# A gated norm and column-scan kernel: the first states, the copies for the median, and the sums at both ends

## What is computed

```
x = x + gate0(gn(x)); x = x + gate1(gn(x)); x = x + gate2(gn(x))   # gn: 32 groups of channels
# gate: mean, max, std of each (image, channel) plane; med = the median of these 3072 values of an image
#   z = sum_k((u - med)**3 * cfc_w) / sqrt(1 + eps) * bn_w + bn_b;  return x * sigmoid(z)
x = x + scan(gn(x))
# scan, step: y = Wc @ prev + conv_b;  y = where(y >= 0, y, prelu_a * y);  cur = y + x_i
#   over the columns forwards (31 steps), then backwards over the result (31 steps)
```

## Time and profile before

| what | us |
|---|---|
| median of three runs | 862.54 (862.22 to 862.80) |
| the profiled execution, its own time | 862.8 |
| its span | 861.1 |
| TensorE busy | 837.6 (97%) |
| VectorE busy | 660.2 (77%) |
| ScalarE busy | 413.6 (48%) |
| GpSimd busy | 67.7 (8%) |

### The profile page before, as it was taken

How to read it: one execution, slowest core, us unless ns; L and a number is a source line. 1 busy time by engine, 2 the same in 40 slices (tenths; PEclk the granted TensorE clock), 3 DMA queues, 4 the chain that set the end, 5 groups by cost and what they waited for, 6 DMA issues and landing times.

```text
span 861.1 us, 13814 instructions
## 1 busy us (share of the span) xinstructions
PE 837.6 (97%) x4062; PEld 662.6 (77%) x4062; DVE 660.2 (77%) x1461; ACT 413.6 (48%) x1375; POOL 67.7 (8%) x106
## 2 busy tenths in 40 slices
PE   7888899999999999999999999999999999999998
PEld 6743478888888888888888888888888888888886
DVE  6977887776766767677776778778787888778887
ACT  6964324544454444544445444544445444454444
POOL 8963300000000000000000000000000000000000
PEclk9999999999999999999999999999999999999999
DMA  9940200000000000000000023332233313332233
GB/s 375 418 188 0 98 26 1 0 0 0 0 0 0 0 0 0 0 0 0 0 0 0 30 68 97 97 97 65 81 97 97 94 58 92 97 97 81 66 97 98
DMA packets 70654, 56.34 MB, mean 65 GB/s; under 512 B 1904, under 2 KB 66416, under 8 KB 68720
## 3 DMA queue, kind: packets, MB, share of 16 engines
q1 hardware_dynamic: 70640, 56.17, 19.6%
HBM read 39.39 MB, written 16.78 MB: 65 GB/s over the span
## 4 chain that ended last, share of the span: by engine, by line
PE 88%; POOL 5%; DVE 4%; ACT 1%; issue 1%; POOLq 0%; DVEq 0%
PE ps_prods L677 27%; PE ps_prods L683 27%; PE ps_prods L680 27%; PE ps_turns L699 6%; POOL pairs L401 3%; ACT stage L500 1%; DVE below_flags L1027 1%; DVE cells L1040 0%; PE ps_below L598 0%; PE ps_values L629 0%; PE ps_group L640 0%; POOL stage L394 0%; POOL stage L397 0%; PE ps_second L662 0%; DVE gate L1082 0%
## 5 line engine op out<-in xcount | busy, mean ns | idle before, releaser
L677 PE MATMUL ps_prods<-w_hi,s_hi 128*128 128x512 f32 (+1 forms) x1000 | 404.6, 405 | 0.2 <-DVE s_hi L1178 0.2
L680 PE MATMUL ps_prods<-w_lo,s_hi 128*128 128x512 f32 (+1 forms) x1000 | 402.7, 403 | 0.0
L683 PE MATMUL ps_prods<-w_hi,s_lo 128*128 128x512 f32 (+1 forms) x1000 | 392.7, 393 | 0.0
L527 ACT ACTIVATE act_buf<-ps_prods 128x256 f32<-128x256 f32 x247 | 81.6, 383 | 352.8 <-PE ps_prods L683 352.8
L1129 DVE SCALAR_TENSOR_TENSOR x_sb<-act_buf,x_sb 128x256 f32 (+1 forms) x247 | 105.2, 426 | 153.6 <-ACT act_buf L534 143.5
L677 PEld LDWEIGHTS ps_prods<-w_hi,s_hi 128*128 128x128 f32 x1000 | 188.4, 188 | 39.5 <-DVE s_lo L1184 1.4
L683 PEld LDWEIGHTS ps_prods<-w_hi,s_lo 128*128 128x128 f32 x1000 | 188.8, 189 | 38.5 <-DVE s_lo L1184 0.2
L680 PEld LDWEIGHTS ps_prods<-w_lo,s_hi 128*128 128x128 f32 x1000 | 189.1, 189 | 32.3
L534 ACT ACTIVATE act_buf<-ps_turns,bias 128x128 f32<-128x128 f32 x494 | 157.0, 377 | 51.6 <-PE ps_turns L699 51.6
L540 ACT ACTIVATE ps_below<-ps_turns,neg_bias 128x128 f32<-128x128 f32 x494 | 152.4, 362 | 0.0
L1136 DVE SCALAR_TENSOR_TENSOR x_sb<-ps_below,neg_slope,x_sb 128x256 f32 (+1 forms) x247 | 118.8, 481 | 5.4
(11 more groups left out here) (198 smaller groups left out, 346.0 us busy)
## 6 DMA issues: line engine op xcount, KB each, us to landing
stage<-x_cols SPq DMA_DIRECT2D x31, 512.0 KB, 4.0
out_cols<-x_sb SPq DMA_DIRECT2D x31, 512.0 KB, 4.8
x_sb<-x_cols SPq DMA_DIRECT2D x15, 1024.0 KB, 19.8
w_raw<-w_t SPq DMA_DIRECT2D x8, 512.0 KB, 19.2
x_sb<-x_cols SPq DMA_DIRECT2D x1, 2048.0 KB, 8.1
x_sb<-x_cols SPq DMA_DIRECT2D x2, 512.0 KB, 27.1
out_cols<-x_sb SPq DMA_DIRECT2D x4, 128.0 KB, 2.1
params<-gates SPq DMA_DIRECT2D x1, 60.0 KB, 14.4
```

The lines of the kernel that those rows point to most:

```text
L527: act.activation(act_buf[:, half], ps_prod[c if bank is None else bank][:, half], ACT.Copy) .then_inc(raw_copied, 1)
L677: pe.matmul(out, s_hi[:, k, :], w_hi[:, k, w_cols], start=(k == 0), stop=False)
L680: pe.matmul(out, s_hi[:, k, :], w_lo[:, k, w_cols], start=False, stop=False)
L683: return pe.matmul(out, s_lo[:, k, :], w_hi[:, k, w_cols], start=False, stop=(k == CT - 1))
```

## The change

The new kernel does these things:

- **Sums of the last tile in parts.** GpSimd adds the first half of the last tile in two pieces too, and TensorE takes each as it comes. ScalarE squares image 0 of the last tile over the columns that landed first, then its last quarter, so there are 33 square passes; VectorE adds the two sums.
- **Copies.** ScalarE makes copies(0) once unit 0 is there, VectorE copies(1) and copies(2); GpSimd none. Two small VectorE instructions of each later layer move into rounds 4 and 5 of the median, and two more of the last norm go.
- **First states.** Before the root is known, ScalarE writes x * a_scale + g_shift for tiles 0 to 5 into stage, 24 instructions of 32 numbers a partition (L541 of the new kernel; g_shift holds pull less the mean until then). VectorE does this for tiles 6 and 7 (L1236, L1238) and multiplies by the root (g_scale until then) into s_hi and stage. TensorE does the s_hi products of a pair ahead of its s_lo products. WARM_UPS is 8.
- **Last two tiles.** Their columns get slope * bias added early (L1181 new), then slope * y (L1151), then (1 - slope) * max(y + bias, 0) (L1157), where max(...) comes from ScalarE.

The diff, cut to its core:

```diff
@@
-    WARM_UPS = 10
+    WARM_UPS = 8
+    RAW_TILES = CT - 2
...
-        act_passes = 1 + N * CT
+        act_passes = 2 + N * CT
@@ block.gpsimd
-                    if ct == CT - 1 and b == 1:
+                    if ct == CT - 1 and b == 0:
+                        pair_add(ct, b, 0, 0, COLS // 4, COLS // 8)
+                        pair_add(ct, b, COLS // 8, COLS // 8, 3 * COLS // 8, COLS // 8)
+                    elif ct == CT - 1:
                         pair_add(ct, b, 0, COLS // 2, 5 * COLS // 8, COLS // 8)
...
+                pool.tensor_scalar(rest_slope[:, :], slope[:, :], -1.0, 1.0, ALU.mult, ALU.add).then_inc(signs_ready, 1)
+                pool.tensor_tensor(sloped_bias[:, :], bias[:, CT - 2:CT], slope[:, 0:1].broadcast_to([P, 2]), ALU.mult)\
+                    .then_inc(signs_ready, 1)
...
-                pool.wait_ge(unit_ready, 2 * layer + 2)
-                pool.tensor_copy(*copies(2)).then_inc(pool_copied, 1)
@@ block.scalar
+                landed = slice(0, LAST_COL if ct == CT - 1 else COLS)
+                plane_square(0, landed, squares_mean[:, 0, ct:ct + 1])
                 if ct == CT - 1:
                     act.wait_ge(x_last_loaded, 16)
-                for n in range(N):
-                    plane_sum(plane_of(n, ct), ACT.Square, squares_mean[:, n, ct:ct + 1], scale=PIX ** -0.5,
-                              bias=mean_div[:, n, ct:ct + 1])
+                    plane_square(0, slice(LAST_COL, COLS), squares_rest[:, 0:1])
+                for n in range(1, N):
+                    plane_square(n, slice(0, COLS), squares_mean[:, n, ct:ct + 1])
...
-                act.wait_ge(unit_ready, 2 * layer + 1)
-                act.activation(*copies(1), ACT.Copy).then_inc(act_copied, 1)
+                act.wait_ge(unit_ready, layer + 1)
+                act.activation(*copies(0), ACT.Copy).then_inc(act_copied, 1)
...
+            act.wait_ge(raw_ready, 1)
+            for ct in range(RAW_TILES):
+                for n in range(N):
+                    rows = slice(n * H, (n + 1) * H)
+                    last = act.activation(stage_col[:, ct, rows], x_sb[:, ct, 0, rows], ACT.Identity,
+                                          bias=g_shift[:, n, ct:ct + 1], scale=a_scale[:, n, ct:ct + 1])
+                last.then_inc(raw_normed, 1)
...
-                act.wait_ge(transposed, final * 4 + 4 + j)
-                act.activation(ps_below[:, 512 + j * P:512 + (j + 1) * P], ps_last_below[j], ACT.Relu,
-                               bias=neg_bias[:, CT - 2 + j:CT - 1 + j], scale=-1.0).then_inc(negated, 1)
+                act.wait_ge(last_turned, j + 1)
+                act.wait_ge(column_added, final * 4 + 7)
+                act.activation(ps_below[:, 512 * j:512 * j + P], ps_last_raised[j], ACT.Relu,
+                               bias=bias[:, CT - 2 + j:CT - 1 + j]).then_inc(negated, 1)
@@ block.tensor
-                    parts = 2 if ct == CT - 1 and b == 1 else 1
+                    parts = 2 if ct == CT - 1 else 1
...
-                        pe.wait_ge(dve_copied, layer + 1)
-                    elif t == 2:
                         pe.wait_ge(act_copied, layer + 1)
-                    elif t == 4:
-                        pe.wait_ge(pool_copied, layer + 1)
+                    elif t % 2 == 0:
+                        pe.wait_ge(dve_copied, 2 * layer + t // 2)
...
-                    pe.transpose(ps_last_below[j], part, ident[:, :])
-                    pe.transpose(ps_last_above[j], part, ident[:, :]).then_inc(transposed, 1)
+                    pe.transpose(ps_last_whole[j], part, ident[:, :]).then_inc(transposed, 1)
+                    pe.transpose(ps_last_raised[j], part, ident[:, :]).then_inc(last_turned, 1)
...
+            def high_products(c, k):
+                w_cols = slice(c * HALF, (c + 1) * HALF)
+                pe.matmul(ps_prod[c], s_hi[:, k, :], w_hi[:, k, w_cols], start=(k == 0), stop=False)
+                pe.matmul(ps_prod[c], s_hi[:, k, :], w_lo[:, k, w_cols], start=False, stop=False)
+
+            def low_product(c, k):
+                return pe.matmul(ps_prod[c], s_lo[:, k, :], w_hi[:, k, c * HALF:(c + 1) * HALF],
+                                 start=False, stop=(k == CT - 1))
...
+                for q in range(1, 4):
+                    pe.wait_ge(first_high, q + 2)
+                    for k in (2 * q, 2 * q + 1):
+                        high_products(0, k)
+                    pe.wait_ge(state_ready, q + 1)
+                    for k in (2 * q, 2 * q + 1):
+                        last = low_product(0, k)
@@ block.vector
+            dve.wait_ge(act_summed, act_passes - (N - 1))
+            whole = mark(dve.tensor_tensor(squares_mean[:, 0, CT - 1:CT], squares_mean[:, 0, CT - 1:CT],
+                                           squares_rest[:, 0:1], ALU.add))
             plane_means(CT - 1).then_inc(means_asked, 1)
...
+                dve.tensor_copy(*copies(1)).then_inc(dve_copied, 1)
+                after(third_unit)
+                dve.tensor_copy(*copies(2)).then_inc(dve_copied, 1)
...
-                dve.tensor_tensor(pull[:, :, :], pull[:, :, :], means, ALU.subtract)
+                dve.tensor_tensor((pull if more else g_shift)[:, :, :], pull[:, :, :], means, ALU.subtract)
...
-                    dve.tensor_tensor(a_scale[:, :, :], a_scale[:, :, :], scaled[:, :, :], ALU.add)
+                    dve.tensor_tensor(a_scale[:, :, :], a_scale[:, :, :], scaled[:, :, :], ALU.add).then_inc(raw_ready, 1)
...
+                        if layer > 0 and k == 4:
+                            dve.tensor_tensor(scaled[:, :, :], a_scale[:, :, :], grow[:, :, :], ALU.mult)
+                        if layer > 0 and k == 5:
+                            dve.tensor_tensor(a_scale[:, :, :], a_scale[:, :, :], scaled[:, :, :], ALU.add)
...
-            def first_state(ct0, cts, shifted, nth, high=None):
+            def first_state(ct0, cts, shifted, nth):
                 part = slice(ct0, ct0 + cts)
+                root = by_row(g_scale, ct0, cts)
+                if ct0 < RAW_TILES:
+                    dve.wait_ge(raw_normed, ct0 + cts)
+                dve.tensor_tensor(by_image(s_hi[:, part, :]), by_image(stage_col[:, part, :]), root, ALU.mult)\
+                    .then_inc(first_high, 1)
+                dve.tensor_tensor(by_image(stage_col[:, part, :]), by_image(stage_col[:, part, :]), root, ALU.mult)\
                     .then_inc(shifted, 1)
...
+            dve.tensor_tensor(g_shift[:, :, :], g_shift[:, :, :], g_scale[:, :, :], ALU.mult)
+            link(dve.tensor_tensor(g_scale[:, :, :], g_scale[:, :, :], a_scale[:, :, :], ALU.mult))
             dve.wait_ge(x_back, 16)
```

More of the change, by code:

```diff
@@ L808, in link @@
                 after(mark(ins))
-            unit_marks = [0]
             def root_seed(out, a):
@@ L880, in first_norm @@
                 means = ps_means.rearrange("p (n c) -> p n c", n=N)
-                after(topped)
+                after(max(topped, whole))
                 dve.wait_ge(off_ready, 2)
@@ L1139, in scan_step @@
                     nth = i * 4 + (2 * c + 5)
+                    if last and c == 1:
+                        dve.wait_ge(signs_ready, 4)
+                        col = column(w, CT - 2, 2)
+                        dve.tensor_tensor(col, col, sloped_bias[:, :].unsqueeze(2).broadcast_to([P, 2, NH]), ALU.add)\
+                            .then_inc(last_sloped, 1)
                     add_above(0)
```

128 lines of the change are left out of this document (63 added, 65 removed).

## The result

The changed kernel takes 853.95 us (853.88 to 854.02), the kernel before on the same chip 862.54 (862.22 to 863.24): a ratio of 0.9897 [0.9886, 0.9907], with the 95% interval in brackets. The prediction was 861.9 with a range of 860.2 to 862.8, so 8 us are missing in it, and the time fell outside the range.

What follows compares the result with a forecast made beforehand. From 116 us on, TensorE's back-to-back products were taken to bound the kernel. Terms 0.0 + 0.61 - 0.49 + 0.50 = 0.62 us gave 862.2 from the profiled execution, 861.9 from the median; range 860.2 to 862.8.

Steps and rivals of the forecast that it cites:

- the interval of ScalarE's instructions: First scan step: start-to-start time of ScalarE's 24 new instructions, taken as 0.29 us, bounds 0.17 and 0.43.
- the covers of the copies: Median copies: whether ScalarE's copy starts sooner than today's; 0.61 us gained if so, range 0.2 to 0.7.
- sums of the last tile: End of the statistics: earlier first piece offset by an added instruction, 0.0 us, bounds -0.1 and +0.15.
- copies: Three layers of the median: six transposes run unbroken without GpSimd's copy, gaining 0.35, 0.18 and 0.08 us.
- first step: First scan step: TensorE starts 0.5 us earlier but then waits for ScalarE, a net loss of 0.49 us.
- last step: Last scan step: last two tiles finish earlier after TensorE's last transposes, gaining 0.50 us.
- both waits: First scan step: TensorE stands about 0.8 us before tiles 2-3 and 0.8 before tiles 4-5.
- 6.18 - 23p: First step's gain in us, p being the interval of ScalarE's 24 instructions; at 0.29 it is -0.49.
- the row-based overlap: First step: profile rows gave each memory operand 0.08 us of interval, so 0.29, against the skill page's 0.306.
- The rival of a free second operand: First step: interval at or below 0.24, gaining 0.6 to 1.36 us; kernel 860.0 to 860.8; chance 0.19.
- that of no overlap: First step: ScalarE's instructions don't overlap, interval towards 0.43, where the kernel takes 865.1 us; chance 0.06.
- none of the three: Besides free operand and no overlap: ScalarE's copy no sooner, VectorE's last four instructions one by one; 862.6 us, chance 0.07.

Runs made afterwards that it cites:

- The run of the change in the old places: Changed kernel with rest_slope and sloped_bias declared behind both_shift, so s_hi, s_lo and act_buf lie as in the kernel before: 862.33 us, ratio 1.0001.
- both runs with TensorE alone: Kernel before plus four steps' products after the last addition, other engines still; old places, then states 128 bytes further: 906.3 and 894.1 us.

## Why the prediction was wrong

**The step that failed** is in its first paragraph: the scan "is TensorE's products back to back, and the change touches none of them but the last few". It holds for their waits and their number, not for their duration: the pitch fell from 232.4 to 228.9 ns, and that is the 8.7 us. No term of the sum had the pitch of the products in it, though the scan is 740 us of the 861: 1% of it is 7 us, more than the four terms together. The chances inherit it. They were spread over the interval of ScalarE's instructions and the covers of the copies, so the range was 2.6 us wide and could not hold the time, and no rival spoke of where the operands lie. The trace of before could not have given the size, since nothing in it has another place for the states. But the change declares two tensors ahead of three that TensorE reads, s_hi, s_lo and act_buf, and that they move could have been seen.

**The sum itself.** In the traces of before and after:

| term | predicted | measured |
|---|---|---|
| sums of the last tile | 0.0 | +0.13 |
| copies | +0.61 (0.35 + 0.18 + 0.08) | +0.60 (0.31 + 0.20 + 0.09) |
| stall in the second layer | none | -0.36 |
| first step | -0.49 | -0.81 |
| last step | +0.50 | +0.49 |
| sum | +0.62 | +0.05 |
| the scan between | 0 | +8.71 |

+0.05 and +8.71 make 8.76, the difference of the spans (861.05 and 852.28). The run of the change in the old places agrees, at 1.0001 [0.9992, 1.0011], though by that interval it could not tell +0.05 from +0.62. Its trace tells more: a_scale is there 0.17 earlier than before (0.37 in the changed kernel), the first step loses 0.84 and the last gives 0.50, so the last two don't come from the places.

*Copies:* right, part by part (the 0.09 of the third layer is what is left of 0.37 - 0.64 when the stall's 0.36 is taken out). *Statistics:* the first piece began at 44.01, 0.34 earlier where I had 0.27; from there to the end of the last read (48.93) lie 4.92 us in place of 4.64, so the further piece cost 0.28, where I had 0.29. VectorE then followed 0.03 behind the read in place of 0.10.

*First step:* the sign, both waits and the mechanism were right; the term mis-sized is the interval, 0.305 in place of 0.29. By the prediction's own formula 6.18 - 23p that is -0.84, measured -0.81. The trace agrees with the Trainium skill here (ScalarE: Activation LUTs, section "What ACT_TABLE_LOAD costs"), which had given 0.306 and, by the prediction, -0.88 (its own formula makes 0.306 come to -0.86); the row-based overlap that I preferred was too generous. The rival of a free second operand is refuted by the same row, and so is that of no overlap. *Last step:* right.

*Rivals:* none of the three came. The faster outcome came by a way that I had no case for.

## What to carry to other kernels

Where one engine is busy 97% of the span with thousands of like instructions, look at their pitch, not only at the waits between them: compare their count in a fixed stretch before and after. A small tensor declared ahead of the operands of a matmul shifts them, and here 64 bytes were worth 1% and 128 bytes 1.4%, more than every edit of the change together. So fix the places of loaded and streamed operands before judging any edit, try one or two placements (here the best was all four at the same place within 256 bytes), and when a diff adds or removes a tensor, undo the shift in a run of its own before crediting the edit.

## What the runs showed of the hardware

- Products of 512 columns with an fp32 128x128 load beside each follow each other every 226.8 ns or every 232.4, by the places of the operands alone, with no other engine at work. In the scan the mean pitch ran from 227.2 ns (the weights by 128 bytes) to 233.5 (s_lo and act_buf by 128).
- The old time came back when the states moved by 256 bytes. The effect is not gradual: 32 bytes beside a good place it is gone.
- The intervals repeat in short turns that run across all kinds of products: seven with the old places, three in the changed kernel.
- After the last addition TensorE had stood idle 1.46 us in both runs with TensorE alone. In one the granted clock stayed at 1.00, its upper level, 2.4 GHz. In the other the first products came at the lower level, 1.2 GHz: a window of them shows 0.55 and they start 0.43 us apart, until 850.47. The same wait did the one and the other, in one execution each.
